# A four-block transformer kernel on one core: router additions between statistics, a shared expert split into z and sigmoid, routing weights spread by TensorE, and a shorter recurrent turn

## The chip, the cores and the metric

The kernel runs on one core of one Trainium2 chip. The metric is device time in microseconds (us) of one execution. A core has five engines that run side by side: TensorE (PE), VectorE (DVE), ScalarE (ACT), GpSimd (POOL) and SyncE (SP, which here issues every DMA). They meet only through semaphores.

## The reference, cut to what matters

Two layers, each an attention-like block and a feed-forward block, each with layer norm in front and a residual sum behind. 2048 tokens of 128 numbers.

```python
x = x + L0_attn(layernorm(x))     # 16 heads of 8, decayed scores, softmax, @ Wo
x = x + L0_ffn(layernorm(x))      # router: 160 experts, the best 8 of each token, and a shared expert
x = x + L1_attn(layernorm(x))     # a 128x128 memory per batch, 16 recurrent chunks of 64 tokens
x = x + L1_ffn(layernorm(x))      # 8 experts, the best 2

# L0_ffn
probs = sigmoid(x @ router_w.T + expert_bias)
top_w, top_idx = top_k(probs, 8);  top_w = top_w / (sum(top_w) + 1e-9) * 2.5
h1w = silu(einsum('th,eih->eti', x, w_gate)) * combine.T[:, :, None]   # combine: top_w at top_idx, 0 elsewhere
routed = einsum('eti,ehi->th', h1w, w_down)
shared = silu(x @ w_gate_shared.T) @ w_down_shared.T

# L1_attn, one chunk
outputs = chunk @ M.T
v_target = mean(silu(outputs @ vg_w1.T) @ vg_w2.T + outputs)
M_new = a * M + b * outer(v_target - M @ k_mean, k_mean)
scale = minimum(MAX_NORM / (norm(M_new) + 1e-6), 1.0)      # MAX_NORM = 30
M = M_new * scale
```

## The kernel before, in words

Each engine's program is written out by hand, in the order in which that engine runs it; every meeting is a semaphore that one engine raises and another waits for. Tokens stand as 16 tiles of 128, in four groups `g` of 512 tokens. The chip's eight accumulator banks (`bank(0)` to `bank(7)`, 128 partitions by 512 floats) are handed round by stage.

**Attention heads.** A loop inside a branch (`If(fast == 1)`; `Else` holds a slower way that these inputs don't take). Behind it `turn_heads(g)` (L1213) transposes a group of head outputs, ACT copies it to `oT` (L980), `projection(g)` (L1331) multiplies by `Wo` into banks 2 and 3, and DVE adds that to `x` (L1816). Projections 0 and 1 stand behind the end of the branch, the heads' second half and projections 2 and 3 behind them.

**First router.** DVE runs `norm(1)`: for group g four statistics and four aggregations (L1616, L1619), POOL works out `rstd` (L676, L677), then DVE writes `xn` of the group before (L1628). PE transposes `xn` (L1142), ACT copies to `xnT` (L856), PE makes the 160 logits of each token (L1355), ACT takes them through Sigmoid (L988) and copies `xh` (L864). DVE picks the best eight of each token (from L1826) and leaves minus the weights in `rest`, which ACT scales, tile by tile (L1020); PE transposes them (L1388, L1389), ACT copies them to `cT_first` (128 experts, L1010) and `cT_last` (32 experts, L1012; the last group's by DVE, L1840). SP stores these rows to DRAM (`c_rows`), waits until they are there, and loads them back, each row spread over 64 partitions, as `cb[u]` (L592, tile `ring`). PE also makes the shared expert's hidden layer (L1369), ACT its Silu (L999), PE its output as the first summand of banks 0 to 3 (L1383).

**Experts' loop.** 80 pairs of experts by four groups: 320 steps. In a step PE makes z into one of banks 4 to 7 (L1401, three matmuls), ACT takes Silu (L1036), DVE multiplies by `cb` (L1858), ACT and DVE split it in two parts `hh` (L1030) and `hl` (L1850), and PE multiplies these by the down weights of earlier steps into banks 0 to 3 (L1414, L1408). `z` of a pair is held in `bank(4 + c % 4)`. The second half of pair 0's `cb` is read first in the third step. After the loop PE finishes the last steps, ACT copies the sums (L1041), PE transposes, DVE adds to `x` (L1864).

**Recurrence.** For 16 chunks `n` and two batches `b`: PE `mz` (L1488) from `state[b]`, a matmul of ones with `m_norm` that sums the squared norm over partitions (L1492), `old` (L1494), outputs (L1499), two matmuls that only keep PE busy (L1152), then, from the sums of silu (ACT L1062), `err` (L1504) and the outputs' second part (L1507). DVE copies the norm (L1921), POOL takes its root (L831), DVE makes `scale` in three small steps (L1933 to L1935), updates `kept` and `state[b]` (L1945) and reduces the squares of `state[1]` (L1948). ACT squares `state[0]`.

## Time and profile before

| | us |
|---|---|
| median of 3 runs | 1076.11 |
| lowest, highest | 1073.52, 1078.62 |
| the profiled execution, its time | 1079.94 |
| its span in the trace | 1078.2 |

The span is what the rows below are measured in, from the first to the last instruction of the profiled execution; its device time is 1.74 us more. Stage borders in the trace: attention until 321, router until 369, experts' loop until 812, second norm until 837, recurrence until 910, last feed-forward to the end.

### The profile page before, as it was taken

How to read it: one execution, taken by the hardware profiler on the slowest of the kernel's cores; microseconds unless marked ns; L12 is line 12 of the kernel's file. 1: busy time of each engine (PE TensorE's matmuls, PEld its weight loads, DVE VectorE, ACT ScalarE, POOL GpSimd, SP SyncE). 2: the span in 40 equal slices, each digit the busy share in tenths (PEclk: the TensorE clock that was granted, in tenths of full speed). 3: DMA queues.
4: the chain of work that ended last, by engine and by line, in shares of the span. 5: the costliest groups of instructions: out<-in, count | busy, mean ns of one | idle time of the engine just before them, and what ended most of it. 6: DMA issues, size and time to landing. Idle time of an engine off the chain costs nothing.

```text
span 1078.2 us, 20266 instructions
## 1 busy us (share of the span) xinstructions
PE 1017.0 (94%) x5239; PEld 687.4 (64%) x5271; DVE 814.9 (76%) x1862; ACT 794.0 (74%) x1327; POOL 232.2 (22%) x355
## 2 busy tenths in 40 slices
PE   5798999999997699999999999999998998999997
PEld 3232333333336378888888888888885777788885
DVE  8544444444447489999999999999996787699997
ACT  5598999999983577887778877778774443565554
POOL 3676864554462000000000000000005111200000
PEclk9899999999998999999999999999999999899999
DMA  4467886776651377777777777776741000034231
GB/s 132 136 196 235 260 257 220 227 232 223 221 198 36 118 283 242 243 242 240 246 243 238 241 234 244 235 249 237 240 125 60 1 2 1 1 110 136 97 108 40
DMA packets 103135, 189.51 MB, mean 176 GB/s; under 512 B 11948, under 2 KB 56620, under 8 KB 103084
## 3 DMA queue, kind: packets, MB, share of 16 engines
q1 hardware_dynamic: 103092, 189.01, 54.2%
q8 instruction: 18, 0.29, 0.1%
q14 instruction: 25, 0.20, 0.1%
HBM read 152.98 MB, written 35.98 MB: 175 GB/s over the span
## 4 chain that ended last, share of the span: by engine, by line
PE 85%; DVE 6%; ACT 3%; POOL 2%; issue 2%; DMA 2%; SPq 0%; DVEq 0%; ACTq 0%; POOLq 0%
PE bank L1401 28%; PE bank L1414 16%; PE bank L1256 11%; PE bank L1408 8%; PE bank L1237 6%; PE bank L1240 5%; PE bank L1504 2%; PE bank L1267 1%; DVE xn L1628 1%; PE bank L1488 1%; POOL m_norm L831 1%; DVE stats L1616 1%; ACT silu_z L1062 1%; PE bank L1142 1%; PE bank L1507 1%
## 5 line engine op out<-in xcount | busy, mean ns | idle before, releaser
L1401 PE MATMUL bank<-xh,w_parts 128*128 128x512 f32 x896 | 278.9, 393 | 1.6 <-DVEq L1844 1.6
L948 ACT ACTIVATE ring<-bank,minus_bound 128x1024 f32<-128x1024 f32 x256 | 262.8, 1119 | 11.0 <-DVE bank L1725 8.1
L1036 ACT ACTIVATE bank<-bank 128x512 f32<-128x512 f32 x320 | 186.2, 582 | 90.8 <-PE bank L1401 90.8
L1858 DVE TENSOR_TENSOR bank<-bank,ring 128x512 f32<-128x512 f32 x320 | 223.9, 700 | 30.3 <-DMA ring<-c_rows 4.2
L1414 PE MATMUL bank<-hh,w_parts 128*128 128x512 f32 x772 | 238.4, 390 | 0.0
L1850 DVE TENSOR_TENSOR hl<-bank,hh 128x512 fp32r<-128x512 f32 x321 | 218.6, 681 | 0.1
L1030 ACT ACTIVATE hh<-bank 128x512 fp32r<-128x512 f32 x321 | 190.8, 594 | 3.9 <-DVE bank L1858 3.8
L1401 PEld LDWEIGHTS bank<-xh,w_parts 128*128 128x128 f32 x896 | 168.9, 190 | 37.9 <-DVEq L1844 1.8
L1725 DVE TENSOR_TENSOR bank<-bank,corner 128x128 f32<-128x128 f32 x256 | 76.4, 298 | 152.2 <-PE bank L1240 149.7
L1401 PE MATMUL bank<-xl,w_parts 128*128 128x512 f32 x448 | 175.7, 392 | 0.0
L1414 PEld LDWEIGHTS bank<-hh,w_parts 128*128 128x128 f32 x772 | 145.4, 188 | 30.5 <-ACT hh L1030 0.4
L1408 PE MATMUL bank<-hl,w_parts 128*128 128x512 f32 x387 | 152.1, 393 | 5.9 <-DVE hl L1850 5.8
L1256 PE MATMUL bank<-ring,v_cur 128*32 128x512 f32 x1024 | 136.4, 605 | 0.1
L1237 PEld LDWEIGHTS bank<-q_stack,k_stack 128*128 128x128 bf16 x320 | 30.3, 97 | 114.7 <-ACT ring L948 93.8
L814 POOL MEMSET q_stack<- 128x512 f32 x2 | 1.0, 530 | 471.0 <-PE bank L1408 471.0
L1237 PE MATMUL bank<-q_stack,k_stack 128*128 128x384 bf16 (+2 forms) x320 | 97.5, 321 | 1.6
L1240 PE MATMUL bank<-q_stack,k_stack 128*128 128x512 bf16 (+3 forms) x352 | 93.3, 325 | 5.0 <-DMA k_stack<-k_parts 3.0
L1401 PEld LDWEIGHTS bank<-xl,w_parts 128*128 128x128 f32 x448 | 84.9, 190 | 18.1
L1408 PEld LDWEIGHTS bank<-hl,w_parts 128*128 128x128 f32 x387 | 72.8, 188 | 24.6 <-DVE hl L1850 9.8
L1113 ACT ACTIVATE q_stack<-bank 128x512 f32<-128x512 f32 x58 | 34.7, 598 | 51.6 <-PE bank L1401 49.7
L2019 DVE TENSOR_TENSOR q_stack<-big,ring 128x512 f32<-128x512 f32 x64 | 44.3, 693 | 12.6 <-ACTq L1093 4.1
L1256 PEld LDWEIGHTS bank<-ring,v_cur 128*32 128x32 f32 x1024 | 20.1, 108 | 48.3 <-ACT ring L948 40.6
(308 smaller groups left out, 1134.5 us busy)
## 6 DMA issues: line engine op xcount, KB each, us to landing
ring<-c_rows SPq DMA_DIRECT2D x174, 512.0 KB, 4.8
w_parts<-w_pairs SPq DMA_DIRECT2D x160, 128.0 KB, 3.2
w_pairs<-xh SPq DMA_DIRECT2D x16, 768.0 KB, 4.4
q_stack<-q_parts SPq DMA_DIRECT2D x64, 144.0 KB
k_stack<-k_parts SPq DMA_DIRECT2D x192, 48.0 KB
w_pairs<-xl SPq DMA_DIRECT2D x16, 512.0 KB, 3.0
big<-in_w_exp SPq DMA_DIRECT2D x16, 384.0 KB, 4.8
w_ffn_parts<-xl SPq DMA_DIRECT2D x16, 384.0 KB, 3.7
```

Of the source, the lines that this page charges most:

```text
L948: act.activation(ring[:, c % RING * S:(c % RING + 1) * S], wide[(m + c) % SB][:], ACT.Exp, bias=minus_bound[:]).then_inc(exp_done, 1)
L1030: act.activation(hh[(c - 1) % 2][:], hidden, ACT.Copy).then_inc(split, 1)
L1036: act.activation(bank(4 + c % ZB), bank(4 + c % ZB), ACT.Silu).then_inc(silu_ready, 1)
L1237: ins = pe.matmul(wide[(m + c) % SB][:, lo:mid], k_stack[0][u][:, keys], q_stack[1][u][:, lo:mid], start=True, stop=True)
L1240: ins = pe.matmul(wide[(m + c) % SB][:, mid:hi], k_stack[1][u][:, keys], q_stack[0][u][:, mid:hi], start=True, stop=True)
L1256: ins = pe.matmul(bank(6 + u)[at:at + 32, :], v_cur[u][:, done_step % QT, :], ring[:, at_ring + h * 512:at_ring + (h + 1) * 512], start=(d ...
L1401: ins = pe.matmul(out_, w[i], x_[j], start=start and k == 0, stop=stop and k == 2, skip_group_check=not start)
L1408: return pe.matmul(bank(done_step % G), w[0], hl[done_step % 2][:], start=False, stop=False, skip_group_check=True)
L1414: ins = pe.matmul(bank(done_step % G), part, hh[done_step % 2][:], start=opens and k == 0, stop=False, skip_group_check=True)
L1725: dve.tensor_tensor(tile, tile, corner[:], ALU.mult).then_inc(corner_done, 1)
L1850: dve.tensor_tensor(hl[(c - 1) % 2][:], hidden, hh[(c - 1) % 2][:].bitcast(F32), ALU.subtract).then_inc(split, 1)
L1858: dve.tensor_tensor(bank(4 + c % ZB), bank(4 + c % ZB), cb[u][:, g * GW:(g + 1) * GW], ALU.mult).then_inc(hid_ready, 1)
```

## The change

1. DVE: `x`'s additions are no longer four in front of the statistics of `norm(1)` and `norm(2)`; each stands directly ahead of its own group's statistics.
2. PE: `projection(0)` and `projection(1)` stand inside both arms of the branch, at their end.
3. Shared expert: its hidden layer is made group by group together with the logits. ACT writes z and sigmoid(z) apart (two copies in place of one Silu, and of another table); DVE multiplies them. Group 0's output is multiplied in the router stage, groups 1 to 3 in the drain behind the experts' loop. Matmuls of `hh` and `hh`, which hold zeros there, clear banks 0 to 3 (`clear_sums`), in place of the idle matmuls L1139 in `norm(1)`.
4. ACT: the scaling of the weights comes behind all four groups of logits, the last group's is done by DVE in one multiplication, and ACT copies `cT_last` of all groups.
5. The weights of pair 0's second half don't go through DRAM: TensorE multiplies `cT_first` by a 0/1 matrix `pair_rows` and ACT copies the result into `cb[0]`. SP loads six blocks less one in front of the loop.
6. Recurrence: the norm is scaled by 1/30^2 in the matmul, so that the scale is one add-and-max and a reciprocal; `state[1]` is updated in two halves with the reduction between them; PE makes the norm between batch 0's and batch 1's `mz`.
7. POOL makes `pair_rows` (two copies of 128 by 64) and one more constant.

```diff
 (sync)
-                sp.wait_ge(cT_ready, min(2 * g + 2, 2 * G - 1))
-                if g == G - 1:
-                    sp.wait_ge(cT_end, 1)
+                sp.wait_ge(cT_ready, 2 * g + 1)
                 sp.dma_start(c_dram[0:P, cols], cT_first[:, cols]).then_inc(c_saved, 16)
+                sp.wait_ge(cT_ready, 2 * g + 2)
                 sp.dma_start(c_dram[P:NE, cols], cT_last[:, cols]).then_inc(c_saved, 16)
                 if g % 2:
                     sp.wait_ge(c_saved, 2 * (g + 1) * 16)
-                    for u in range(2):
+                    for u in range(g // 2, 2):
                         load_rows(u, u, g // 2)
 (scalar)
             def take_group(g):
+                act.wait_ge(shared_psum, g + 1)
+                act.activation(shared_z[g][0:EI], bank(2 + g % 2)[0:EI, :], ACT.Copy)
+                act.activation(shared_hid[g][0:EI], bank(2 + g % 2)[0:EI, :], ACT.Sigmoid).then_inc(shared_act, 1)
                 take_logits(g)
                 high_x(g, 1)
...
+            def take_spread(k):
+                act.wait_ge(spread_psum, k + 1)
+                ins = act.activation(cb[0][:, (2 + k) * GW:(3 + k) * GW], bank(6 + k), ACT.Copy)
+                if k:
+                    ins.then_inc(cb_loaded[0], 16)
...
+            scale_chosen(0)
+            scale_chosen(1)
+            act.activation(early_table[:], half[:, 0:1], ACT.Silu)
+            take_cT(0)
+            scale_chosen(2)
+            take_cT(1)
+            take_cT(2)
+            take_cT(3)
+            take_spread(0)
+            take_spread(1)
 (tensor)
-            norm(1, router_logits, 4)
-            pe.wait_ge(x_ready, G)
+            def tokens_of(g):
+                pe.wait_ge(xnT_ready, G + g + 1)
+                shared_hidden(g)
+                router_logits(g)
+            norm(1, tokens_of)
+            def clear_sums(times):
+                for g in range(times * G):
+                    pe.matmul(bank(g % G), hh[0][:, 0:P], hh[1][:], start=True, stop=False, skip_group_check=True)
+            pe.wait_ge(shared_act, G)
+            clear_sums(4)
+            pe.wait_ge(gate_ready, G)
+            def shared_sum(g):
+                pe.wait_ge(shared_ready, g + 1)
+                return pe.matmul(bank(g), wd_shared[:], shared_hid[g][0:EI], start=False, stop=False, skip_group_check=True)
...
+            for k in range(2):
+                pe.wait_ge(cT_ready, 2 * (3 + k))
+                pe.matmul(bank(6 + k), pair_rows[:], cT_first[:, (2 + k) * GW:(3 + k) * GW], start=True, stop=True).then_inc(spread_psum, 1)
...
+                    if c == 2:
+                        pe.wait_ge(cb_loaded[0], 16)
...
             for c in range(2):
                 down_low(turn_ - 3 + c, down(turn_ - 3 + c), MT_N * G - 3 + c, hl_ready, CREDIT + 1).then_inc(low_used, 1)
+                if c == 0:
+                    shared_sum(1)
                 down_high(turn_ - 2 + c, down(turn_ - 2 + c), MT_N * G - 2 + c, hh_ready).then_inc(down_done, 1)
+                shared_sum(2 + c)
...
-                pe.matmul(bank(6)[:, 256:256 + B], ones[:], m_norm[:, 0, :], start=True, stop=True).then_inc(norm_psum, 1)
-                for b in range(B):
+                    if b == 0:
+                        if n:
+                            pe.wait_ge(rows_ready, n)
+                            pe.wait_ge(side_ready, B + 5 * (n - 1) + 1)
+                        pe.matmul(bank(6)[:, 256:256 + B], across(norm_unit[:], P), m_norm[:, 0, :], start=True, stop=True).then_inc(norm_psum, 1)
 (vector)
-            norm(1)
+            norm(1, add_projection)
+            def shared_product(g):
+                dve.wait_ge(shared_act, g + 1)
+                dve.tensor_tensor(shared_hid[g][0:EI], shared_hid[g][0:EI], shared_z[g][0:EI], ALU.mult).then_inc(shared_ready, 1)
+            shared_product(0)
...
-            norm(2)
+            norm(2, add_experts)
...
-                        link(dve.tensor_scalar(m_norm[:, 3, :], m_norm[:, 2, :], 1e-6, None, ALU.add))
-                        link(dve.reciprocal(m_norm[:, 3, :], m_norm[:, 3, :]))
-                        dve.tensor_scalar(m_norm[:, 3, :], m_norm[:, 3, :], MAX_NORM, 1.0, ALU.mult, ALU.min)\
-                            .then_inc(scale_ready, 1)
+                        link(dve.tensor_scalar(m_norm[:, 3, :], m_norm[:, 2, :], 1e-6 / MAX_NORM, 1.0, ALU.add, ALU.max))
+                        dve.reciprocal(m_norm[:, 3, :], m_norm[:, 3, :]).then_inc(scale_ready, 1)
```

How the order moves, at three places. First ACT in the router stage, between the last logits and the first transposed weights. Before (L1020 scales the weights, L1010 and L1012 copy their transposes, L999 is the shared expert's Silu):

```order
L864 ACTIVATE xh<-xnT 128x512 [waits xnT_ready]
L999 ACT_TABLE_LOAD [waits shared_psum]
L999 ACTIVATE q_stack<-bank 64x512 [waits moe_zero]
L999 ACTIVATE q_stack<-bank 64x512 [waits shared_psum]
L1020 ACTIVATE ring<-ring,top_inv 128x160 [waits combine_ready]
L1020 ACTIVATE ring<-ring,top_inv 128x160 x3
L1010 ACTIVATE xn<-bank 128x512 [waits cT_psum]
L1012 ACTIVATE fold<-bank 32x512
L999 ACTIVATE k_stack<-bank 64x512 [waits shared_psum] x2
L1020 ACTIVATE ring<-ring,top_inv 128x160 [waits combine_ready]
```

Now (L1001 and L1002 take z and sigmoid, L995 the logits, L1029 scales, L1034 loads Silu's table, L1015 and L1016 copy the transposes):

```order
L1001 ACTIVATE evac<-bank 64x512 [waits shared_psum]
L1002 ACTIVATE k_stack<-bank 64x512
L995 ACTIVATE big<-bank 128x640 [waits logit_psum]
L871 ACTIVATE xh<-xnT 128x512 [waits xnT_ready]
L1029 ACTIVATE ring<-ring,top_inv 128x160 [waits combine_ready]
L1029 ACTIVATE ring<-ring,top_inv 128x160 x3
L1029 ACTIVATE ring<-ring,top_inv 128x160 [waits combine_ready]
L1029 ACTIVATE ring<-ring,top_inv 128x160 x3
L1034 ACT_TABLE_LOAD
L1034 ACTIVATE early_table<-half 128x1
L1015 ACTIVATE xn<-bank 128x512 [waits cT_psum]
L1016 ACTIVATE fold<-bank 32x512
```

The shared expert's work has moved ahead of the scaling, into each group of logits, and two groups are scaled before the first transpose is copied.

Second, PE at the entry to the experts' loop. Before:

```order
L1388 MATMUL bank<-ident,ring 128x128 [waits scaled_ready,cT_ready]
L1389 MATMUL bank<-ident,ring 32x128
L1388 MATMUL bank<-ident,ring 128x128 [waits scaled_ready]
L1389 MATMUL bank<-ident,ring 32x128
L1424 UNCONDITIONAL_BRANCH [waits xl_ready,cT_end,moe_zero,cT_ready,parts_loaded3]
```

Now (L1424 and L1425 are the transposes, L1433 spreads pair 0's weights, L1443 is z):

```order
L1424 MATMUL bank<-ident,ring 128x128 [waits combine_ready,cT_ready]
L1425 MATMUL bank<-ident,ring 32x128
L1433 MATMUL bank<-xn,pair_rows 128x512 [waits cT_ready] x2
L1466 UNCONDITIONAL_BRANCH [waits xl_ready,moe_zero,cT_ready,parts_loaded3]
L1443 MATMUL bank<-xh,w_parts 128x512 [waits hl_ready]
L1443 MATMUL bank<-xh,w_parts 128x512
```

Two matmuls that read the last copied weights now stand between the last transposes and the loop.

Third, DVE in a recurrent turn. Before, from the update of the states to the scale:

```order
L1945 SCALAR_TENSOR_TENSOR state<-bank,steps,ring 128x256 [waits err_psum0,dve_link]
L1945 SCALAR_TENSOR_TENSOR state<-bank,steps,ring 128x256 [waits err_psum1]
L1948 ISA m_sq,m_norm<-state 128x128 [waits state_ready1]
L1948 ISA m_norm 128x1
L1921 COPY m_norm<-bank 128x2 [waits norm_psum]
L1916 SCALAR_TENSOR_TENSOR big<-bank,m_norm,out_sum 128x64 [waits side_ready] x2
L1927 SCALAR_TENSOR_TENSOR ring<-bank,steps,ring 128x256 [waits side_ready,old_psum0]
L1933 TENSOR_SCALAR m_norm<-m_norm 128x2 [waits out_taken1,out_taken0,norm_ready]
L1934 RECIPROCAL m_norm<-m_norm 128x2 [waits dve_link]
L1935 TENSOR_SCALAR m_norm<-m_norm 128x2 [waits dve_link]
```

Now:

```order
L2005 SCALAR_TENSOR_TENSOR state<-bank,steps,ring 128x256 [waits err_psum0,dve_link]
L2005 SCALAR_TENSOR_TENSOR state<-bank,steps,ring 128x128 [waits err_psum1]
L2009 ISA m_sq,m_norm<-state 128x128 [waits state_ready1]
L2009 ISA m_norm 128x1
L2005 SCALAR_TENSOR_TENSOR state<-bank,steps,ring 128x128
L1982 COPY m_norm<-bank 128x2 [waits norm_psum]
L1977 SCALAR_TENSOR_TENSOR big<-bank,m_norm,out_sum 128x64 [waits side_ready] x2
L1988 SCALAR_TENSOR_TENSOR ring<-bank,steps,ring 128x256 [waits side_ready,old_psum0]
L1994 TENSOR_SCALAR m_norm<-m_norm 128x2 [waits out_taken1,out_taken0,norm_ready]
L1995 RECIPROCAL m_norm<-m_norm 128x2 [waits dve_link]
```

The second batch's update is in two halves with the reduction (L2009) between them, and one of the three small steps to the scale is gone.

## Rows read from the trace of the kernel before

**Rows 1.** PE by stretch: busy time, clock granted, DMA share, GB/s

```profile
380.00:382.00 2.00, 2.00 (x7) 0.55 1.02 412
400.00:800.00 400.00, 400.00 (x1765) 1.00 0.73 238
```

**Rows 2.** Chain that ended last, 316 to 382 us (start us, length us, what)

```profile
321.42 2.90 issue
...
368.61 4.43 DMA c_rows<-fold
373.06 4.32 DMA ring<-c_rows
```

**Rows 3.** Timeline of the router stage: start, us, engine, line, tiles, idle before

```profile
329.92 0.69 DVE L1816 TENSOR_TENSOR x<-x,bank 128x512 f32<-128x512 f32 x1 [2.23 <-PE bank L1331]
...
336.63 1.11 DVE L1628 TENSOR_SCALAR xn<-x,mv,rstd 128x128 f32<-128x128 f32 x4
...
338.91 1.11 DVE L1628 TENSOR_SCALAR xn<-x,mv,rstd 128x128 f32<-128x128 f32 x4
...
340.29 0.70 ACT L988 ACTIVATE big<-bank 128x640 f32<-128x640 f32 x1 [0.69 <-PE bank L1355]
...
340.57 1.45 DVE L1628 TENSOR_SCALAR xn<-x,mv,rstd 128x128 f32<-128x128 f32 x4 [0.54 <-POOL rstd L677]
...
341.94 1.00 DVE L1826 MAX8 top<-big 128x8 f32<-128x160 f32 x4
...
344.09 0.70 ACT L988 ACTIVATE big<-bank 128x640 f32<-128x640 f32 x1 [0.49 <-PE bank L1355]
...
350.24 1.28 ACT L999 ACT_TABLE_LOAD   x1
...
352.51 1.37 ACT L1020 ACTIVATE ring<-ring,top_inv 128x160 f32<-128x160 f32 x4
```

**Rows 4.** Timeline of the way into the experts' loop

```profile
355.55 0.82 DVE L1836 SCALAR_TENSOR_TENSOR ring<-ring,big 128x640 f32<-128x640 f32 x1
...
359.85 1.98 PE L1383 MATMUL bank<-q_stack,wd_shared 64*128 64x512 f32 x4
...
368.39 0.48 DVE L1843 MEMSET bank<- 128x512 f32 x1 [0.24 <-DVE fold L1840]
...
369.01 0.73 PE L1401 MATMUL bank<-xh,w_parts 128*128 128x512 f32 x2 [1.57 <-DVEq L1844]
...
377.49 0.70 DVE L1858 TENSOR_TENSOR bank<-bank,ring 128x512 f32<-128x512 f32 x1 [4.22 <-DMA ring<-c_rows]
```

**Rows 5.** Timeline of DVE in the experts' loop, ninth step

```profile
386.86 0.70 DVE L1858 TENSOR_TENSOR bank<-bank,ring 128x512 f32<-128x512 f32 x1
```

**Rows 6.** Timeline of the drain of the experts' loop

```profile
810.14 0.51 PE L1408 MATMUL bank<-hl,w_parts 128*128 128x512 f32 x1
...
812.31 0.46 PE L1408 MATMUL bank<-hl,w_parts 128*128 128x512 f32 x1
...
812.81 2.07 ACT L1041 ACTIVATE big<-bank 128x512 f32<-128x512 f32 x4 [1.32 <-PE bank L1408]
```

**Rows 7.** Timeline of one recurrent turn

```profile
863.16 0.88 DVE L1945 SCALAR_TENSOR_TENSOR state<-bank,steps,ring 128x256 f32<-128x256 f32 x2 [0.25 <-PE bank L1504]
...
864.07 0.29 DVE L1948 CUSTOM_DVE_ANT_0 m_sq<-state 128x128 f32<-128x128 f32 x1
...
864.43 0.38 PE L1492 MATMUL bank<-m_norm,ones 128*128 128x2 f32 x2
...
865.98 0.71 PE L1152 MATMUL bank<-xh 128*128 128x512 f32 x2
...
866.22 0.17 DVE L1935 TENSOR_SCALAR m_norm<-m_norm 128x2 f32<-128x2 f32 x1
...
866.42 0.31 ACT L1062 ACTIVATE silu_z<-bank,m_norm 128x64 f32<-128x64 f32 x1 [1.32 <-DVE m_norm L1935]
...
866.88 0.91 PE L1504 MATMUL bank<-vg_cat,h_sum 128*128 128x256 f32 x3 [0.18 <-ACT silu_z L1062]
```

More of the change, by code:

```diff
@@ L213, in build @@
         shared_hid = act_out + [k_stack[0][u][:].bitcast(F32) for u in range(2)]
+        shared_z = [k_stack[1][u][:].bitcast(F32) for u in range(2)] + [evac[u][:] for u in range(2)]
         hid = [q_stack[1][u][:].bitcast(F32) for u in range(2)]
@@ L659, in _ @@
             link(pool.memset(ones[:], 1.0))
+            link(pool.memset(norm_unit[:], 1.0 / (MAX_NORM * MAX_NORM)))
             link(pool.memset(m_norm[:], 0.0))
@@ L1010, in take_cT, with scale_chosen @@
                 act.activation(cT_first[:, cols], bank(4 + g % 2), ACT.Copy).then_inc(cT_ready, 1)
-                if g < G - 1:
-                    act.activation(cT_last[:, cols], bank(6 + g % 2)[0:NE - P, :], ACT.Copy).then_inc(cT_ready, 1)
-            for g in range(G):
-                if g < 2:
-                    take_shared(2 * g)
-                    take_shared(2 * g + 1)
+                act.activation(cT_last[:, cols], bank(6 + g % 2)[0:NE - P, :], ACT.Copy).then_inc(cT_ready, 1)
+            def take_spread(k):
[3 more added lines that the diff above has]
+                    ins.then_inc(cb_loaded[0], 16)
+            def scale_chosen(g):
                 act.wait_ge(combine_ready, g + 1)
@@ L1205, in _, with projection @@
             pe.matmul(bank(6)[:, 0:1], ones[0:1, :], bound[0:1, 1:2], start=True, stop=True).then_inc(bound_psum, 1)
+            def projection(g):
+                pe.wait_ge(oT_ready, g + 1)
+                if g >= 2:
+                    pe.wait_ge(x_ready, g - 1)
+                for t in range(TPG):
+                    ins = pe.matmul(bank(2 + g % 2)[:, t * P:(t + 1) * P], oT[:, g * GW + t * P:g * GW + (t + 1) * P], wo[:],
+                                    start=True, stop=True)
+                ins.then_inc(y_psum, 1)
             def turn_heads(g):
@@ L1323, in _ @@
                 turn_heads(1)
-            def projection(g):
-                pe.wait_ge(oT_ready, g + 1)
-                if g >= 2:
-                    pe.wait_ge(x_ready, g - 1)
-                for t in range(TPG):
-                    ins = pe.matmul(bank(2 + g % 2)[:, t * P:(t + 1) * P], oT[:, g * GW + t * P:g * GW + (t + 1) * P], wo[:],
-                                    start=True, stop=True)
-                ins.then_inc(y_psum, 1)
-            projection(0)
-            projection(1)
+                projection(0)
+                projection(1)
             pe.wait_ge(o_all, 1)
@@ L1460, in token_scalars @@
                 if g < G - 1:
-                    spare(7, 2)
+                    spare(4, 2)
                 pe.wait_ge(xnT_ready, 2 * G + g + 1)
@@ L1604, in _, with norm @@
             link = Link(dve, dve_link)
-            def norm(k):
+            def norm(k, make_x=None):
                 for g in range(G + 1):
@@ L1812, in _, with add_projection @@
                 dve.sem_inc(o_all, 1)
-            for g in range(G):
+            def add_projection(g):
                 ts = slice(g * TPG, (g + 1) * TPG)
@@ L1860, in _, with add_experts @@
             low_part(MT_N * G, 0, bank(4 + ZB - 1), hh_ready, low_used, hl_ready)
-            for g in range(G):
+            def add_experts(g):
                 ts = slice(g * TPG, (g + 1) * TPG)
```

90 lines of the change are left out of this document (49 added, 41 removed).

## The prediction, made before the changed kernel ran

> **What bounds the kernel now.** I read the busy times by stretch first. In the experts' loop PE is busy 400.00 of 400 us with 1765 matmuls, 0.227 us each; a step has six, 1.36 us, and nothing in the change removes one of the 320 steps [rows 1]. So the change can only act on what stands outside that loop. There I read the chain that ended last and then the timelines of each place. Before the loop the chain crosses an idle PE that waited for nothing the profile shows, 2.90 us behind the heads, and then runs through the router. The first loop steps hang on two DMA trips, 4.43 us for the last store of the routing weights and 4.32 us for the reload [rows 2]. Logits pass at 3.80 us a group (340.29 to 344.09), the picking of the best eight begins at 341.94 [rows 3], and its last result is there at 356.37, but PE enters the loop only at 369.01 and DVE stands still 4.22 us in front of the third step, until 377.49 [rows 4]. In the recurrence the chain goes round once a turn, from the silu through PE, DVE, PE, DVE, POOL and DVE to the next silu [rows 7].
>
> **Start of the router stage (parts 1 and 2).** The third addition starts at 329.92, held by the second half of the heads, behind which it waited 2.23 us [rows 3]. Projections 0 and 1 now run where PE idled for its 2.90 us, and the idle stretch of the branch comes behind them [rows 2]; heads and projections 2 and 3 come when they came, so I anchor the third addition at 330.0. The gain is on DVE: groups 0 and 1 are added and measured while DVE waited. From the anchor: addition 0.7, then one statistics-and-xn round of 2.28 (336.63 to 338.91), addition 0.7, another 2.28, then 0.54 of waiting and 1.4 for the last xn [rows 3], together 7.9: xn done at 337.9 in place of 341.94.
>
> For the branch the Trainium skill has a rule, "Advanced Engine Details and Errata", section "Control Flow Timing": some 0.05 us for an unconditional and 0.11 for a comparing branch. The trace shows 2.90 us at this place and I go by the trace; were the rule the whole cost, it would make a case of its own (fourth rival).
>
> **Picking and scaling (parts 3 and 4).** Four groups take from 341.94 to 356.37, 3.61 each [rows 3, 4]. In front stands the shared product of group 0, 0.6 (half the partitions of the 0.70 rows, the same columns) [rows 4]: groups end at 342.1, 345.7, 349.3 and 352.9, and the last has one more pass over 640 columns, 0.83 like L1836 [rows 4]: 353.8. Do logits keep up? ACT's group has two 512-column copies more, 0.5 each: four of one shape took 2.07 [rows 6]. But PE drops the four idle matmuls of a group, about 0.9, for the shared matmul, about 0.9 by half of 1.98 us for four records [rows 4]. I take 3.85 a group from a first gate at 336.6, the last at 346.4: DVE is the later one. ACT then scales groups 0 and 1 from 347 (1.1 each, less than the single 1.37 because they overlap [rows 3]), loads Silu's table 1.28 [rows 3], copies group 0 (1.0), scales group 2 (1.1), copies groups 1 and 2 (2.0). This ends near 355, and PE's transposes of group 3 (0.9) end near 355.7; with ACT's copies the last weights are out at 357.1, against 368.3, a tenth before the memset of 368.39 [rows 4].
>
> For the table load the skill states more ("ScalarE: Activation LUTs", "What ACT_TABLE_LOAD costs"): about 1.38 us of draining behind the 1.28, 2.66 in all. The row shows 1.28 and the Silu of the same line began at once; by the page the entry would come 1.4 later, by the row nothing is added. I take the row.
>
> **Entry to the loop (part 5).** New on the path: the second spread matmul, 0.9, waits for those last weights; ACT's copy 0.6 with two hand-overs of 0.2; then the memset 0.48 and 0.14 to the first matmul (368.39 to 369.01) [rows 4]. So PE enters at 357.1 + 2.5 = 359.6; I write 360.0, for hand-overs. DVE's subtraction and three products behind 353.8, 4.3 in all, end at 358.1, just ahead. Bounds for the spread: nothing if it hid, twice the matmuls' time (+0.9) at the half clock. Gain at the entry: 9.0.
>
> Pair 0's second half is in place when the loop starts, so the 4.22 us stop goes. Without it the third step would have stood at 373.3, the ninth at 381.5; it stood at 386.86 [rows 4, 5]: 5.35, of which 1.1 is the half clock behind the stop: PE's granted clock is 0.55 at 380 to 382 [rows 1], the lower level of 1.2 GHz for most of it. What is late next is pair 1's second half: store and reload (4.43 + 4.32 [rows 2]) put it at about 366.5, and it is read in the seventh step, 361.6 + 8.2 = 369.8: 3.3 to spare. With a second c_saved wait in front of it (1 MB of loads is then still under way) I allow 2 of these. The new wait for `cb_loaded[0]` on PE stands in every third step of sixteen, always met after the first.
>
> So the ninth step gains 9.0 + 5.35 = 14.35. I take 0.85 off for one stretch of half clock somewhere in the new, thinner PE schedule, a little less than the 1.1 that the one behind the stop cost. **Router: -13.5.** Bounds: -8 if ACT's group takes 5 us, -16 if nothing dips.
>
> **Drain (part 3's other end).** From the third-last low matmul, 810.14, to the last, 812.31, are 2.17 us; between them stand two low and two pairs of high, 6 x 0.227 = 1.36, so 0.8 is idle. Three shared matmuls bring six records of about 0.43, 2.56 (1.98 for four, less the tail of the last) [rows 4, 6]. Idle time hides 0.8: the accumulators are ready 1.75 later. ACT's copies at 812.81, the DVE additions and all behind wait for that. **Drain: +1.75**, bounds +0.9 (if high and shared overlap better) and +2.6 (nothing hidden).
>
> **Second norm (part 1).** The additions arrive at DVE's own pace and DVE works without a gap, so mixing them in changes the order, not the sum. First xn comes earlier, the last is bound by the same work. Only a wait of the kind of the 0.54 shrinks. **-0.1**, bounds -1.3 (all of the two additions moved past the first xn) and +0.3.
>
> **Recurrence (part 6).** One small step less is 0.20 (866.22 to 866.42) [rows 7]. The split: two 256-column updates take 0.88, so one has 0.40 of pitch and 0.48 of length; a 128-column one ends 0.13 earlier, and the reduction at 864.07, with the norm matmul at 864.43, moves by that [rows 7]. 0.33 a turn. The second batch's `mz`, moved behind the norm, puts about 0.25 (two records, estimate) between the norm and the two idle matmuls: these began 1.55 behind the norm and the next `err` 2.45 behind it [rows 7]. Now 1.80, plus 0.45 for the two, is 2.25, and `err` would be called for at 2.45 - 0.20 = 2.25. It just fits; one term more on PE and it is the bound. Fifteen turns have both: **-5.0**, bounds -2 (PE binds) and -5.6.
>
> [...] Idle matmuls moved to another bank: same count.
>
> **Sum.** -13.5 + 1.75 - 0.1 - 5.0 = -16.9, on the profiled execution's 1079.94: 1063.0. That execution is 3.8 above the median of 1076.11, so for a median I say 1059.5.
>
> **Rivals.**
> - PE or ACT binds the router (two more copies and one more fp32 matmul in each group, at half clock). Against it: 3.80 a group before with matmuls of the same length [rows 3]. From 5 us a group on, gates and not DVE set the pace: four groups 1.2 later each, +5: 1064.5. Chance 0.12.
> - The recurrent turn doesn't shorten, because PE's queue behind the norm takes over (the 2.25 against 2.25 above). Then -16.9 becomes -12.9: 1063.5. Chance 0.12.
> - Slower: a step of the loop grows. PE has no gap there (400.00 of 400 [rows 1]), and its third step of each sixteen now waits on one more semaphore. To eat 16.9 us in 20 such steps each would have to cost 0.85; from there on the kernel is slower. At 1.2 us a wait, +24: 1083. Nothing in the rows speaks for it; the wait for loaded weights, which is of the same kind, leaves no gap. Chance 0.02.
> - The idle PE behind the branch isn't the branch's. Then heads and projections 2 and 3 come 2.9 earlier than I have them, with all behind: 1056.6. By the skill's rule on branches this would be so; against it stands the 2.90 itself [rows 2]. Chance 0.06.
> - The change does little: spreading and clearing eat what DRAM cost, the entry gains only 3: 1068. Chance 0.04.
>
> The forecast itself has 0.64, and within its own mechanism 1056.5 to 1062.5. The range takes the rivals on both sides and a median that can lie 2.5 off: 1054 to 1066.5. Half a per cent, 5.4 us, is about what this measurement tells from no change: faster is below 1070.7. Faster 0.95, within 0.03, slower 0.02.
>
> **What would show it.** Entry: PE's first loop matmul near 360, DVE without a gap before the third step, no long stop at the seventh. Last xn of the first norm near 338; each pick still 3.6. Drain: the last low matmul 1.75 later against the loop's end. Turn: silu to silu 4.2 in place of 4.5, with PE's idle matmuls ending where `err` begins. The prediction is wrong if gates come later than picks, if pair 1's weights are late at the seventh step, if the granted clock stays low over the entry, or if a turn stays above 4.4.

## The result, and the profile after

The changed kernel takes 1062.08 us (median of 4 runs, 1061.62 to 1064.72), the kernel before beside it 1076.49 (4 runs): ratio 0.9878, 95% interval 0.9857 to 0.9900. The forecast was 1059.5 us, range 1054 to 1066.5, and faster. A second set of runs gave 0.9878 again (0.9858 to 0.9899). The execution profiled took 1062.44, its span 1060.7.

PE by stretch, after. The experts' loop is untouched (400.00 of 400 us), and the half clock behind the old stop is gone, 1.00 where [rows 1] have 0.55:

```profile
380.00:382.00 2.00, 2.00 (x10) 1.00 1.04 409
400.00:800.00 400.00, 400.00 (x1753) 1.00 0.70 229
```

The chain that ended last, after, against [rows 2]. Two stops of "issue" stand where there was one, then all goes through ACT until two DMA trips:

```profile
319.20 2.81 issue
322.02 1.51 PE bank L1242 x6
323.53 1.91 issue
325.44 0.59 PE bank L1242 x2
...
345.63 2.55 ACT ring L1029 x8
348.20 1.28 ACT L1034
...
352.91 3.28 DMA c_rows<-fold
356.20 4.42 DMA ring<-c_rows
```

Timeline of DVE and ACT in the router, after, against [rows 3]. The first `xn` begins before addition 2; the third addition ends a wait of 1.16; picks follow each other at 3.58 (336.44, 340.02), gates at 4.08 but ahead of them:

```profile
325.56 1.11 DVE L1677 TENSOR_SCALAR xn<-x,mv,rstd 128x128 f32<-128x128 f32 x4
327.84 0.69 DVE L1866 TENSOR_TENSOR x<-x,bank 128x512 f32<-128x512 f32 x1 [1.16 <-PE bank L1232]
...
333.97 0.70 ACT L995 ACTIVATE big<-bank 128x640 f32<-128x640 f32 x1 [0.21 <-PE bank L1376]
...
334.47 1.45 DVE L1677 TENSOR_SCALAR xn<-x,mv,rstd 128x128 f32<-128x128 f32 x4 [0.54 <-POOL rstd L681]
...
336.44 0.99 DVE L1882 MAX8 top<-big 128x8 f32<-128x160 f32 x4
...
338.05 0.70 ACT L995 ACTIVATE big<-bank 128x640 f32<-128x640 f32 x1 [0.21 <-PE bank L1376]
```

Timeline of the way into the loop, after, against [rows 4, 5]: spread matmuls, memset, PE's entry at 358.07, the first, third, seventh and ninth step of DVE. The 4.22 us stop is gone; two small ones on the DMA, 2.13 at the first step and 0.47 at the seventh, are there:

```profile
355.10 2.09 PE L1433 MATMUL bank<-xn,pair_rows 128*128 128x512 f32 x4 [0.28 <-ACT fold L1016]
...
358.07 0.73 PE L1443 MATMUL bank<-xh,w_parts 128*128 128x512 f32 x2 [0.89 <-DVEq L1905]
358.12 0.48 DVE L1904 MEMSET bank<- 128x512 f32 x1 [2.19 <-ACT ring L1021]
...
360.74 0.70 DVE L1919 TENSOR_TENSOR bank<-bank,ring 128x512 f32<-128x512 f32 x1 [2.13 <-DMA ring<-c_rows]
...
363.14 0.69 DVE L1919 TENSOR_TENSOR bank<-bank,ring 128x512 f32<-128x512 f32 x1
...
368.91 0.70 DVE L1919 TENSOR_TENSOR bank<-bank,ring 128x512 f32<-128x512 f32 x1 [0.47 <-DMA ring<-c_rows]
...
371.32 0.69 DVE L1919 TENSOR_TENSOR bank<-bank,ring 128x512 f32<-128x512 f32 x1
```

Timeline of the drain, after, against [rows 6]. From the third-last low matmul to the last it is 5.15 where it was 2.17. A shared sum holds PE 1.05 until the next matmul begins (795.21 to 796.26, 798.87 to 799.92). A line of the trace of before stands first; it names a wait inside the 2.17:

```profile
811.50 0.19 PEld L1408 LDWEIGHTS bank<-hl,w_parts 128*128 128x128 f32 x1 [0.52 <-DVE hl L1850]
```

```profile
794.77 0.51 PE L1450 MATMUL bank<-hl,w_parts 128*128 128x512 f32 x1
...
795.21 1.12 PE L1414 MATMUL bank<-q_stack,wd_shared 64*128 64x512 f32 x2
...
796.26 0.73 PE L1456 MATMUL bank<-hh,w_parts 128*128 128x512 f32 x2
796.92 0.29 PEld L1414 LDWEIGHTS bank<-k_stack,wd_shared 64*128 64x128 f32 x2 [0.36 <-issue]
...
798.87 1.12 PE L1414 MATMUL bank<-k_stack,wd_shared 64*128 64x512 f32 x2
799.92 0.49 PE L1450 MATMUL bank<-hl,w_parts 128*128 128x512 f32 x1
```

Timeline of a recurrent turn, after, against [rows 7]: from silu to silu 4.18. PE's idle matmuls (L1171) are over just before `err` (L1551), which still waits 0.19 for the silu:

```profile
853.77 0.70 PE L1171 MATMUL bank<-xh 128*128 128x512 f32 x2
853.79 0.31 ACT L1081 ACTIVATE silu_z<-bank,m_norm 128x64 f32<-128x64 f32 x1 [0.99 <-DVE m_norm L1995]
...
854.24 0.73 PEld L1551 LDWEIGHTS bank<-vg_cat,h_sum 128*128 128x128 f32 x4 [0.19 <-ACT silu_z L1081]
...
857.97 0.31 ACT L1081 ACTIVATE silu_z<-bank,m_norm 128x64 f32<-128x64 f32 x1 [0.99 <-DVE m_norm L1995]
```

**One yardstick for all traces.** The last heads' transposes on PE (320.60 before, 316.76 after) lie ahead of everything that the change touches on PE, ACT and DVE (POOL's two small copies, 0.42 us together, end 4.3 us earlier), and their time varies from execution to execution. So I measure each stage from its own start: H is that transpose; xn the start of the first router's last `xn`; entry PE's first loop matmul; ninth DVE's ninth step, all three less H; drain from the third-last low matmul to the last; norm 2 from ACT's copies of the accumulators to the first silu; turns from the first silu to the last; rest from addition to the end of the span. All experiments are in it.

```
kernel (profiled run)    H       xn     entry  ninth  drain  norm 2 turns  rest
before                 320.60   19.97   48.41  66.26  2.17   26.39  68.44  168.1
after                  316.76   17.71   41.31  54.56  5.15   28.21  63.29  166.3
after again            318.61   17.10   40.73  53.61  5.15   26.95  63.32  167.9
turn alone             318.51   19.83   46.94  62.09  2.16   26.07  63.42  166.2
norm 2 adds first      318.48   17.22   40.83  54.51  5.16   26.08  63.35  167.9
sums ahead             318.83   16.70   42.22  54.75  2.16   26.91  63.35  166.2
rows by DRAM           318.68   17.73   40.02  61.06  5.15   27.21  63.32  166.3
projections behind     316.59   16.67   40.26  54.48  5.15   26.85  63.33  166.3
norm 1 adds first      318.08   21.70   47.72  60.74  5.15   27.08  63.32  166.4
norm 2 busy            318.43   17.49   41.09  54.12  5.15   26.45  63.29  166.2
sums in router         318.03   16.91   39.62  53.94  2.17   26.82  63.41  166.3
three edits            318.19   16.87   42.30  54.80  2.16   26.09  63.32  166.2
all edits              320.71   16.55   39.26  52.18  2.17   26.09  63.39  166.2
```

### The profile page after: what moved, and what is told of

Same layout as the page of the kernel before. It is cut to its first block, busy times and chain, and to the rows that moved or that the text cites. A ratio compares the mean times of both kernels' runs of the same rounds, so it can differ in the third digit from the quotient of the medians.

```text
span 1060.7 us, 20364 instructions
## 1 busy us (share of the span) xinstructions
PE 1013.6 (96%) x5287; PEld 685.9 (65%) x5287; DVE 816.6 (77%) x1865; ACT 796.0 (75%) x1331; POOL 233.1 (22%) x358
## 4 chain that ended last, share of the span: by engine, by line
PE 87%; DVE 4%; ACT 2%; POOL 2%; issue 2%; DMA 1%; SPq 0%; DVEq 0%; POOLq 0%; ACTq 0%
PE bank L1443 29%; PE bank L1456 16%; PE bank L1285 12%; PE bank L1450 8%; PE bank L1269 6%; PE bank L1266 6%; PE bank L1541 1%; PE bank L1296 1%; PE bank L1171 1%; DVE xn L1677 1%; DVE state L2005 1%; PE bank L1551 1%; PE bank L1161 1%; PE bank L1546 1%; DVE stats L1665 1%
## 5 line engine op out<-in xcount | busy, mean ns | idle before, releaser
L1443 PE MATMUL bank<-xh,w_parts 128*128 128x512 f32 x896 | 277.7, 391 | 0.9 <-DVEq L1905 0.9
L1443 PEld LDWEIGHTS bank<-xh,w_parts 128*128 128x128 f32 x896 | 167.9, 189 | 37.7 <-DVEq L1905 1.7
L1443 PE MATMUL bank<-xl,w_parts 128*128 128x512 f32 x448 | 174.9, 390 | 0.0
L1269 PE MATMUL bank<-q_stack,k_stack 128*128 128x512 bf16 (+3 forms) x384 | 98.7, 330 | 4.4 <-DMA k_stack<-k_parts 2.8
L1443 PEld LDWEIGHTS bank<-xl,w_parts 128*128 128x128 f32 x448 | 84.5, 189 | 17.9
```

What stands on the lines that cost most here:

```text
L1269: ins = pe.matmul(wide[(m + c) % SB][:, mid:hi], k_stack[1][u][:, keys], q_stack[0][u][:, mid:hi], start=True, stop=True)
L1443: ins = pe.matmul(out_, w[i], x_[j], start=start and k == 0, stop=stop and k == 2, skip_group_check=not start)
```

## The experiments

The runs came in three sets, each with its own runs of the kernel before (1076.54, 1075.47 and 1077.45 us). Ratios are to these.

**The turn alone.** The kernel before with part 6 only, the split update and the shorter scale with it. The edit, cut to the norm matmul:

```diff
-                pe.matmul(bank(6)[:, 256:256 + B], ones[:], m_norm[:, 0, :], ...)
+                    if b == 0:
+                        pe.matmul(bank(6)[:, 256:256 + B], across(norm_unit[:], P), m_norm[:, 0, :], ...)
```

> The kernel before with the shorter recurrent turn alone (part 6). My theory: 15 turns of 4.19 us in place of 4.52, 5.0 us less in the recurrence and nothing elsewhere, so 1071.4 against 1076.5, ratio 0.9953. Rival (the whole gain is the router's and noise): ratio 1.000 and the same turn.

Measured: 1070.62 us, ratio 0.9942 (0.9919 to 0.9965), 5.9 us less; in its trace the turns take 63.42 against 68.44, 5.02 less. The turn is worth what was forecast. Its router is the old one, yet H to the ninth step takes 62.09 where the profile of before had 66.26: the third step waits 1.24, not 4.22.

```profile
372.83 0.70 DVE L1860 TENSOR_TENSOR bank<-bank,ring 128x512 f32<-128x512 f32 x1 [1.24 <-DMA ring<-c_rows]
```

So the same code differs by 4 us between two executions, and this one (1066.45) was the fastest of its seven.

**Second norm's additions in front.** The changed kernel, that place as before.

```diff
-            norm(2, add_experts)
+            for g in range(G):
+                add_experts(g)
+            norm(2)
```

> The changed kernel with norm(2)'s additions in front of its statistics again. In the profile of the changed kernel the stretch from the accumulators' copy to the first silu took 28.2 us against 26.4 before, with TensorE granted 0.50 from 810 to 816, behind 2.35 us without a matmul between group 0's and group 1's xn. Theory A: mixing the additions opens that gap and so brings the half clock; without it the stretch is 26.4 again and the kernel 1.8 us faster than the changed one. Rival B: the half clock there is chance; the stretch differs from 28.2 by less than 0.5, or is 26.4 in both when the changed kernel is run again.

Measured: 1064.45 us, 0.9882 (0.9857 to 0.9907): no gain in the time. In the trace its stretch takes 26.08 in place of 28.21, but the six other executions with mixed additions and nothing else changed at that place take 26.82 to 27.21 there. So 0.7 to 1.1 us of the stretch come with the mixed additions each time, and the rest of those 2.1 us was one execution's.

**Shared sums ahead of the loop.** None is left for the drain.

```diff
+            for g in range(1, G):
+                shared_sum(g)
...
-                if c == 0:
-                    shared_sum(1)
...
-                shared_sum(2 + c)
```

> The changed kernel with the shared expert's sums 1 to 3 between the spread matmuls and the experts' loop, none in the drain. Theory A: each such sum costs 1.0 us wherever nothing hides it; the drain from third-last to last low matmul falls from 5.15 to 2.17 us, and the loop starts 2.3 later (3.15 less 0.89 of idle), together -0.7 against the changed kernel. Rival B: in the drain they cost only my 1.75, so the drain falls by that and the kernel is 0.5 slower.

Measured: 1060.74 us, 0.9840 (0.9808 to 0.9871). The drain is 2.16 again, PE enters 0.9 to 1.5 later, and the ninth step comes only 0.2 to 1.1 later: at the changed kernel's entry the first step waited for the DMA anyway.

**Rows by DRAM.** Pair 0's weights all take the way of before.

```diff
-                    for u in range(g // 2, 2):
+                    for u in range(2):
...
-            for k in range(2):
-                pe.wait_ge(cT_ready, 2 * (3 + k))
-                pe.matmul(bank(6 + k), pair_rows[:], cT_first[:, (2 + k) * GW:(3 + k) * GW], ...)
```

> The changed kernel, but all of pair 0's weights go through DRAM as before: no spread matmuls, no copies of them. Theory A: the loop starts 2.0 earlier, but the third step waits again for store and reload, about 8.7 us behind the last store, so that it stands some 5 us later than in the changed kernel: +4 to +5 us in all. Rival B: the reload is hidden well enough by now (the rows of the first half came late as well), and it is within 1 us.

Measured: 1071.50 us, 0.9938 (0.9915 to 0.9961), 8.1 to 9.4 above the changed kernel's two medians (one of them from another set), and 6.5 by the ratios to each set's own runs of before (0.9938 against 0.9878). PE enters as early as ever (40.02), but the third step waits longer than before the change:

```profile
369.60 0.70 DVE L1912 TENSOR_TENSOR bank<-bank,ring 128x512 f32<-128x512 f32 x1 [5.06 <-DMA ring<-c_rows]
```

The third step stands 4.5 to 5.4 later behind H, as expected. The ninth comes 6.5 to 7.5 later, which agrees with the ratios: behind the stop PE's granted clock is 0.50 from 369.2 to 376.0, where the changed kernel has 1.00. So theory A holds for the stop; what it left out, 2.0 us or more behind the third step, fits this half clock.

**The changed kernel again.**

> The changed kernel, unaltered, beside the four others of this call. Theory: the 3.84 us that the changed kernel was ahead at the last heads' transposes (316.76 against 320.60) and the 1.8 us in the last part of the program are chance of one execution, since no line there was changed. Then the last transposes of a second profile lie anywhere from 316.5 to 321, the stretch from them to the ninth loop step is again near 54.6, the drain again 5.15 from the third-last to the last low matmul, and the median is 1062 to 1064. Rival: the kernel's new layout of code or buffers moves something in front of the router; then the heads come at 316 to 317 again.

Measured: 1063.43 us, 0.9878 (0.9858 to 0.9899); H at 318.61, ninth 53.61, drain 5.15. The first theory holds: H wanders from 316.6 to 320.7 over the table, and the rest takes either 166.3 or 168 whatever the kernel. The traces show what the 1.7 us of the rest hang on. PE was granted half clock for 6.8 us somewhere between 910 and 934 in the three executions with 167.9 to 168.1 (before at 926.3, this one at 910.3, "norm 2 adds first" at 910.0), and in that part for 3.4 us or not at all in the ten with 166.2 to 166.4.

**Projections behind the branch.** As before on PE.

```diff
                 turn_heads(0)
                 turn_heads(1)
-                projection(0)
-                projection(1)
...
+            projection(0)
+            projection(1)
```

> Projections 0 and 1 stand behind the branch on PE again, all else as changed. Theory: in the changed kernel PE stands still twice behind the branch, 2.81 us and then 1.91 us in the middle of the heads, where the kernel before stood once (3.07), since there the 2.66 us of projections lay between; and addition 0 is held by DVE's own branch, not by the projection. Then addition 0 stays 4.9 us behind the last transposes, the second stop goes, addition 2 comes at 9.9 in place of 11.1, and the last xn 1.1 earlier: 0 to 1.5 us faster than the changed kernel in the stretch from the transposes to the ninth step. Rival (the prediction's own step): the projections filled an idle PE, and behind the branch they cost DVE the 2 us again: additions 1 to 1.5 later, last xn 1 to 2 later.

Measured: 1064.28 us, 0.9892 (0.9866 to 0.9917), no difference from the changed kernel. PE of this kernel stops once:

```profile
319.96 2.76 PE L1232 MATMUL bank<-wo,big 128*128 128x128 f32 x16 [2.71 <-issue]
322.51 1.91 PE L1242 MATMUL bank<-ident,o_heads 128*128 128x128 f32 x8
```

Addition 2 comes at 10.04 behind H in place of 11.08 (10.46 in the second execution), the last `xn` 1.04 earlier (0.43 against the second execution). The first theory had both. Addition 0 stays at 5.05 (4.84 and 5.34 in the changed kernel); the trace names PE as what ended its wait here and DVE's own "issue" there, so the two arrive at about the same time. But the ninth step stays (54.48): the first step now waits 2.35 and the seventh 1.25 for the DMA.

**First norm's additions in front.** As before on DVE, all else changed (the same edit for `norm(1, add_projection)`).

> All four additions stand in front of the first router's statistics again, the rest as changed. Theory: DVE then works off all statistics behind addition 3, as before (9.75 us from addition 3 to the last xn), and addition 3 stays held by PE at about 12 behind the transposes: last xn 21.9 in place of 17.7, the ninth step 3 to 4.2 later, median 3 to 4 above the changed kernel's. Rival: the gates and picks are not bound by xn, and the loop's entry hangs on the DMA of the weights, so that 1 us or less comes out at the ninth step.

Measured: 1070.11 us, 0.9950 (0.9927 to 0.9973), 6.7 above the changed kernel in the same set, where 3 to 4 were expected. The last `xn` is 4.0 to 4.6 later as worked out. The rest comes from the gates: with `xn` late the chain through PE and ACT is uncovered, and DVE waits for it at the first three groups of picks, of which two are shown:

```profile
342.41 1.01 DVE L1884 MAX8 top<-big 128x8 f32<-128x160 f32 x4 [0.50 <-ACT big L995]
...
346.49 1.01 DVE L1884 MAX8 top<-big 128x8 f32<-128x160 f32 x4 [0.40 <-ACT big L995]
```

The first two groups of picks then take 4.08 each, ACT's pace, and not 3.58: the last group begins 5.65 later behind H than in the changed kernel, PE enters the loop 6.4 to 7.0 later. This is the rival "ACT binds". It needs no 5 us a group, as the prediction had it: 4.08 is enough once the first `xn` is late, and the early first `xn` is what holds it off in the changed kernel (first gates 17.21 behind H, first picks 19.68).

**Sums in the router, products on GpSimd.** The four shared sums take the place of the idle clearing matmuls.

```diff
-            shared_product(0)
...
+            for g in range(3):
+                shared_sum(g)
```

> The shared products run on GpSimd and all four shared sums on PE inside the router, as the accumulators' first writes in place of the idle clearing matmuls; none is left for the drain. Theory: the drain goes back from 5.15 to 2.17 from the third-last to the last low matmul, as with the sums ahead of the loop; the picks begin 0.7 earlier, since DVE has no product in front; PE enters the loop 0.3 to 0.7 earlier than the changed kernel. In all 3 to 3.7 below the changed kernel, 1058.5 to 1059.5. Rival: a GpSimd product of 64 rows and 512 columns takes several times DVE's 0.68 and shares its access to memory, so that the picks slow down or PE waits for the products: then the entry comes up to 2 later and only 1 to 2 us are left of the gain.

Measured: 1060.32 us, 0.9850 (0.9826 to 0.9873), 3.1 below the changed kernel in the same set. The drain is 2.17. The rival has its share in the router: GpSimd's product takes 1.26 against DVE's 0.68, DVE's last `xn` beside it 1.99 against 1.45, and the first three groups of picks take 3.80, 4.08 and 3.63, so nothing comes of the product that DVE no longer does. The picks themselves are not slower. In each of these three groups one small `tensor_scalar`, 0.17 in the changed kernel, takes 0.38, 0.66 and 0.22, and ends 0.03 or 0.04 behind the end of GpSimd's instruction; the second of four instructions of `xn` begins as the product ends, at 336.08:

```profile
334.81 1.27 POOL L816 TENSOR_TENSOR q_stack<-q_stack,k_stack 64x512 f32<-64x512 f32 x1
334.94 1.99 DVE L1679 TENSOR_SCALAR xn<-x,mv,rstd 128x128 f32<-128x128 f32 x4 [0.54 <-POOL rstd L681]
336.85 0.99 DVE L1883 MAX8 top<-big 128x8 f32<-128x160 f32 x4
...
342.44 1.26 POOL L816 TENSOR_TENSOR k_stack<-k_stack,evac 64x512 f32<-64x512 f32 x1 [2.82 <-ACT k_stack L1005]
343.08 0.66 DVE L1890 TENSOR_SCALAR top_sum<-top_sum 128x4 f32<-128x4 f32 x1
```

**PE busy in the second norm.** The changed kernel with eight idle matmuls ahead of group 1.

```diff
+                    if k == 2 and g == 1:
+                        spare(4, 8)
```

> The changed kernel with eight idle matmuls on PE between groups 0 and 1 of the second norm, where it stood still 2.35 us. From the accumulators' copies to the first silu the changed kernel took 28.21 and 26.95 us in two executions, with the additions in front 26.1 to 26.4. Theory 1: the surplus is the half clock that PE falls to behind its idle stretch; then the granted clock is 1.00 from 806 to 818 and the stretch takes 26.1 to 26.4. Theory 2: about 0.75 of it is the order of DVE's work and only the rest the clock; then the stretch takes 26.8 to 27.0 at full clock. Rival: the idle matmuls delay the transposes behind them, and the stretch takes 27.5 or more. The whole: 0 to 2 us below the changed kernel, hardly to be told.

Measured: 1062.05 us, 0.9872 (0.9839 to 0.9905), as the changed kernel. PE by stretch, of the changed kernel and then of this one:

```profile
810.00:814.00 4.00, 3.87 (x9) 0.50 0.01 2
814.00:818.00 4.00, 4.00 (x14) 0.71 0.00 0
```

```profile
810.00:814.00 4.00, 2.83 (x12) 1.00 0.01 2
814.00:818.00 4.00, 3.65 (x16) 1.00 0.00 0
```

The stretch takes 26.45 at full clock. Of it 0.38 is DVE's: from ACT's copies to the last `xn` 13.16, as in the changed kernel, against 12.78 with the additions in front. So both theories have a part: 0.4 is the order of the work, the rest (0.4 to 1.8) PE at its lower level of 1.2 GHz behind an idle stretch. The other traces agree. The changed kernel's profile has 6.8 us at half clock here and takes 28.21; the six others with mixed additions and PE idle for 2.35 us have 3.4 us of it and take 26.82 to 27.21; this one, and the five with the additions in front, have none and take 26.45 and 26.07 to 26.39.

**Three edits** (sums ahead, projections behind, second norm's additions in front) and **all edits** (the same with the sums in the router and products on GpSimd).

> The changed kernel with three edits: shared sums ahead of the loop, projections 0 and 1 behind the branch on PE, and the second norm's additions in front of its statistics. Theory, by the single edits: sums -2.8 (drain 2.17 again, 0.2 lost at the entry), projections 0 to -0.4 (the first steps hang on the DMA), second norm -0.75: 3.5 to 4 below the changed kernel's 1062.1 to 1063.4, at 1059. Rival: the loop's entry, 0.9 later with the sums in front, is now the later one against the DMA, and what the projections bring shows in full: -4.5 to -5, 1058.

> As the kernel with three edits, but the shared products on GpSimd and the sums inside the router in place of idle matmuls. Theory: -3.1 for those as measured, -0.75 for the second norm, 0 to -0.4 for the projections' place: 1058.5 to 1059.5, and the first loop step waits 3.5 to 4 us for the routing weights' DMA, so that an earlier entry brings nothing. Rival: additions one after the other in the second norm lose what the idle PE gained, and only the -3.1 stays: 1060.

Measured: 1062.11 us, 0.9859 (0.9828 to 0.9890), and 1059.67 us, 0.9846 (0.9814 to 0.9878). The five ratios with sums left in the drain and the new router order lie between 0.9872 and 0.9892, the four with the sums out of it between 0.9840 and 0.9859: about 3 us, the size of the drain's term. The intervals of the two families overlap at the edge (0.9859 has 0.9828 to 0.9890), but in each of the four traces the drain is 3.0 shorter. Between those four the runs can't choose. The fastest by its median is the one with all edits.

## Why the prediction was right, step by step

**Total.** The forecast was 2.6 us too low, 3.9 against the second median (1063.43), which lies outside its own mechanism's range (1056.5 to 1062.5) while the first is just inside. In the terms of the two profiled executions: router -11.7 for -13.5, drain +2.98 for +1.75, second norm +1.8 for -0.1, turns -5.15 for -5.0: -12.1 for -16.9. The drain (at most +2.6) and the second norm (at most +0.3) came out beyond their own bounds, and all three misses go the same way. That the profiled time came to 1062.44, beside the 1063.0 of the sum, is luck: 3.84 lay ahead of H and 1.8 behind the last addition, in code that the change left alone; for the 1.8, before had PE at half clock for 6.8 us there and after for 3.4.

**Start of the router.** The step that failed is the anchor, "heads and projections 2 and 3 come when they came". With the projections out of the way PE enters the heads 0.9 earlier than before (5.25 behind H for 6.17), runs six matmul records and stops again for 1.91, so that projection 2 begins 1.14 later than before. It and projection 3 then run mostly at half clock (granted 0.50 from 321.4 to 328.2) and take 3.10 for 2.26. Addition 2 came 11.08 behind H and not 9.4. From it to the end of the last `xn` 8.08 were measured and 7.9 forecast. The lateness stands at 1.8 at the first pick (19.68 for 17.9) and at the last, and at 1.9 at the entry (41.31 for 39.4); in size it is the router's miss. As an order, part 1 is right and worth more than I gave it: 6.7 us, shown by undoing it. Projections ahead of the branch's end, to which I gave the idle PE, bring nothing that the runs can tell: undoing them costs nothing. Addition 0 was held in the changed kernel by a stop of DVE's own, 3.01 us of "issue".

On branches the Trainium skill ("Advanced Engine Details and Errata", "Control Flow Timing") gives 0.05 and 0.11 us. PE's first stop was 1.9 to 3.2 in the 13 traces, the second 1.7 to 2.9 where there was one. The rival by that rule, 1056.6, is out; the trace disagrees with the rule as the whole cost.

What ends these stops can be read from the DMA records of the packed traces, which hold the transfers of 16384 bytes on the instruction queue, q8. At all 21 stops of the 13 traces PE goes on 1.2 to 1.6 us behind the end of such a transfer. In the changed kernel's profile they run from 319.50 to 320.43 and from 322.92 to 324.10, and PE goes on at 322.02 and 325.44. With projections 0 and 1 behind the branch the second transfer comes just as soon (321.17 to 322.09 in that kernel's trace, 3.6 behind the first), but PE still has projections and the heads' transposes to run, until 324.4, and does not stop. So the stops fit a wait for the next instructions; that is read from the times alone, and no run changed the transfers.

**Picks, scaling, table load.** 3.58 a group for 3.61, gates at 4.08 for 3.85 and still ahead. The table load is 1.28 and the next activation begins at 349.50, 0.02 behind: the row was right. The Trainium skill's 1.38 more did not show ("ScalarE: Activation LUTs", "What ACT_TABLE_LOAD costs").

**Entry.** From last pick to entry 6.35 for 6.2, but by two errors that nearly cancel. The last copy of weights ended 39.25 behind H where 36.5 was forecast: 1.8 of that is the lateness above and 1.0 ACT's queue, whose scaling took 1.3 a group and not 1.1, and which waited 1.09 for group 2's transposes. From there to the entry it took 2.06 and not 2.9, since PE did not wait for the memset (358.07 and 358.12). The 0.85 set aside for a half clock was not needed for that, the granted clock is 1.00 from 350 to 372; it was used up by the two stops on the DMA. The stop at the third step is gone, shown by putting the DRAM way back (+6.5 by the ratios, 8.1 to 9.4 by the medians). What I missed is pair 0's first half: its rows (groups 0 and 1) wait for ACT, which first has four groups of gates, so they are stored at 352.9 and back at 360.7, where DVE waited 2.13 for them. And pair 1's second half, with "3.3 to spare", was 0.47 late. It landed 52.15 behind H and not 45.9: the last copy was 2.75 late; SP, held by its wait for the first stores, issued the last store 3.1 after it (359.10 behind 356.01); store and wait took 5.4, not 4.43, and the reload 0.1 more; the forecast had 0.65 in hand. PE's entry and the weights for the first and the seventh step now arrive close together, and so the 1 us of the projections and the 0.9 of the sums ahead of the loop both vanished. My 5.35 for the old stop was one execution's: another had 1.24 in place of 4.22 at that step.

**Drain.** Right mechanism, wrong size: 1.05 and not 0.85 for a shared sum, and 0.17 hidden, not 0.8. Both sizes were the pitch inside a run of one kind of matmul. Inside a run of fp32 records it is 0.43, two make 0.85; with the experts' matmuls before and behind (their inputs are of another type, fp32r), the first record holds PE 0.53 and the second 0.52. And the six fp32r records between the sums, 1.36 at 0.227 each, took 1.99 (0.44, 0.66, 0.33 and 0.56). The trace of before does name waits in the 2.17, so the idle time was real; but what the sums hid of it the changes of kind took back. Removing the sums took the drain back to 2.17 and some 3 us off the time.

**Second norm.** "Changes the order, not the sum" failed: four additions in a row take 2.48, one at a time 0.72 each until the next instruction, the statistics that wait for its result: 0.4 more. PE then stood idle 2.35 us in one piece, and was at half clock behind that, another 0.4 to 1.8.

**Turn.** 4.18 for 4.2, the fit of PE's idle matmuls against `err` as worked out. Shown alone: 5.0 in the trace, 5.9 by the medians, and the ratio's interval (3.8 to 8.7 us) holds 5.0. The prediction's price for the rival here doesn't close: -12.9 leaves 1 us of gain for the turns, where the bound of the same case leaves 2.

**POOL's copies.** The sum has no term for POOL's two copies of `pair_rows`. They take 0.42 us together (at 312.04, 43 us ahead of the spreading), and no wait in the trace names them.

## What to carry to other kernels

Measure each stage from a landmark in unchanged code, since here differences before and behind the change came to 5.6 us between two profiles, and read the granted clock of each stage with its time. When a stop is removed, work out the next arrival of every partner at that place (here ACT's queue and SP's, not the DMA's duration alone); where three arrivals lie within 1 us, a single edit shows nothing. Work that moves into an idle place is hidden only if it costs there what it cost elsewhere: here a matmul of another kind among those of the drain made both dearer, and of 0.8 us of idle time 0.17 was left to gain.

## What the runs showed of the hardware

- Behind the branch PE stood still 1.9 to 3.2 us in all 13 traces. With the heads' transposes next in its program it stood again, six matmul records later, for 1.7 to 2.9 us (8 traces of 8); with the 16 records of projections 0 and 1 next (2.6 us of work and more), it did not (5 of 5). At all 21 stops it went on 1.2 to 1.6 us behind the end of a 16384-byte transfer on the instruction queue.
- A 64-row fp32 product of 512 columns takes 1.26 us on GpSimd (0.68 on DVE). Beside it DVE's `tensor_scalar` instructions were held until it ended (`xn` 1.99 for 1.45, a 128x4 one 0.38 and 0.66 for 0.17), while MAX8 and MATCH_REPLACE8 kept their times (0.99 or 1.00 for four, 0.31).
- The two fp32 matmul records of 512 columns of a shared sum (64 rows) hold PE 1.05 us among fp32r matmuls in the drain, and 0.43 each in a run of their own kind. The spreading's first two (128 rows) hold it 0.96, 0.53 and 0.43, as the same places in a run of 64 rows do in "sums ahead".
- PE was granted half clock for 3.4 or 6.8 us at a time. In the second norm, behind an idle stretch of 2.35, 3.4 us of it cost 0.4 to 0.8 us and 6.8 us of it 1.8. In the last part of the program the executions with 6.8 us of it took 1.7 us longer than those with 3.4 or none.
- Storing 512-token rows to DRAM and loading them spread takes 3.28 + 4.42 us for groups 0 and 1, and 5.4 + 4.4 for groups 2 and 3, beside other loads (DMA share 0.29 from 350 to 358 and 0.68 from 358 to 366).
